# A decoder layer on one core: the last batch's attention finished in two pieces, with alternating PSUM banks

## The reference

```python
gating = jax.nn.softmax(x @ W_gate.T, axis=-1)
idx = jnp.argmax(gating, axis=-1)                 # one of 16 heads per token
k_shared = ...                                    # the chosen head's key, 16 wide
v_shared = ...                                    # its value times its gate
att = jnp.einsum('bhqd,bkd->bhqk', q, k_shared) * (1.0 / math.sqrt(hd))
att = jax.nn.softmax(jnp.where(causal[None, None, :, :], att, -jnp.inf), axis=-1)
y = jnp.einsum('bhqk,bkd->bhqd', att, v_shared)   # 16 heads, one key and value for all
x = _layernorm(x + y, axis=-1)
```

## Time and profile before

| what | value |
|---|---|
| median of 3 runs | 359.49 us (357.77 to 359.7) |
| the profiled execution's own time | 355.84 us |
| its span, first to last instruction | 353.7 us |
| TensorE busy | 315.0 us (89%) |
| VectorE busy | 258.7 us (73%) |
| ScalarE busy | 218.1 us (62%) |
| GpSimd busy | 202.1 us (57%) |
| mean granted TensorE clock | 0.979 |

### The profile page before, as it was taken

How to read it: one execution, slowest core, us unless ns; L and a number is a source line. 1 busy time by engine, 2 the same in 40 slices (tenths; PEclk the granted TensorE clock), 3 DMA queues, 4 the chain that set the end, 5 groups by cost and what they waited for, 6 DMA issues and landing times.

```text
span 353.7 us, 6078 instructions
## 1 busy us (share of the span) xinstructions
PE 315.0 (89%) x2016; PEld 237.1 (67%) x2016; DVE 258.7 (73%) x494; ACT 218.1 (62%) x664; POOL 202.1 (57%) x285
## 2 busy tenths in 40 slices
PE   0949799999999999999999999977779999999972
PEld 0846588778868868877877877855455666666641
DVE  2773984874885794795794595799977989998643
ACT  3638547747655756657657655552347778777781
POOL 0487562775681684582585584299893567922112
PEclk9978999999999999999999999999989999999997
DMA  7921010013000004100004000000000000000001
GB/s 254 330 99 59 3 31 2 1 40 140 1 21 11 2 1 125 56 0 30 2 0 131 1 1 2 0 3 0 0 2 2 2 0 17 19 16 17 0 17 44
DMA packets 5615, 13.06 MB, mean 37 GB/s; under 512 B 849, under 2 KB 3025, under 8 KB 5329
## 3 DMA queue, kind: packets, MB, share of 16 engines
q1 hardware_dynamic: 5040, 11.90, 10.1%
q10 hardware_dynamic: 544, 0.79, 0.7%
HBM read 11.63 MB, written 1.05 MB: 36 GB/s over the span
## 4 chain that ended last, share of the span: by engine, by line
PE 67%; DVE 12%; POOL 10%; issue 5%; DMA 2%; ACT 2%; SPq 1%; POOLq 0%; DVEq 0%; ACTq 0%
PE bank L346 12%; PE bank L467 11%; PE bank L377 8%; PE bank L363 7%; PE bank L456 5%; POOL q_rope L290 4%; DVE toep L999 4%; PE bank L625 4%; PE bank L445 3%; PE bank L614 3%; POOL q_rope L293 3%; PE bank L580 3%; PE bank L635 2%; DMA anti<-in_anti 2%; DVE t_cos L964 2%
## 5 line engine op out<-in xcount | busy, mean ns | idle before, releaser
L1357 POOL TENSOR_TENSOR prob<-prob,rden 128x512 f32<-128x512 f32 x32 | 33.6, 1051 | 69.6 <-DVE rden L1026 69.6
L1336 POOL TENSOR_TENSOR t_sin<-rot,sin 128x512 f32<-128x512 f32 x40 | 54.4, 1360 | 26.4 <-ACT rot L738 23.5
L768 ACT ACTIVATE prob<-bank,neg_max 128x128 f32<-128x128 f32 x128 | 45.3, 369 | 39.1 <-DVE neg_max L1019 39.1
L346 PE MATMUL bank<-x_hi,w_hi 128*128 128x512 f32 x96 | 36.8, 466 | 8.6 <-ACT w_hi L719 8.2
L377 PEld LDWEIGHTS bank<-k_rope,q_rope 128*128 128x128 f32 x256 | 35.0, 200 | 10.5 <-DVE q_rope L977 5.1
L467 PE MATMUL bank<-wo_hi,head_hi 128*128 128x256 f32 x128 | 39.1, 305 | 2.8 <-DVE head_lo L1062 2.7
L377 PE MATMUL bank<-k_rope,q_rope 128*128 128x128 f32 x256 | 35.6, 284 | 4.7 <-DVE q_rope L977 4.7
L894 ACT ACTIVATE prob<-bank,fneg_max 128x128 f32<-128x128 f32 x128 | 36.7, 380 | 2.6 <-DVE fneg_max L1240 2.6
L467 PE MATMUL bank<-wo_lo,head_hi 128*128 128x256 f32 x128 | 36.0, 281 | 0.0
L467 PE MATMUL bank<-wo_hi,head_lo 128*128 128x256 f32 x128 | 35.9, 281 | 0.0
L1326 POOL TENSOR_TENSOR kv<-ctxT 128x256 f32<-128x256 f32 (+3 forms) x64 | 35.2, 585 | 0.0
(11 more groups left out here) (104 smaller groups left out, 743.2 us busy)
## 6 DMA issues: line engine op xcount, KB each, us to landing
w_raw<-in_wqkv SPq DMA_DIRECT2D x3, 768.0 KB, 5.5
toep<-in_toep SPq DMA_DIRECT2D x8, 256.0 KB, 3.3
wo_raw<-in_wo SPq DMA_DIRECT2D x4, 512.0 KB, 3.6
x_raw<-in_xt SPq DMA_DIRECT2D x2, 512.0 KB, 5.9
ctxT<-in_ctx SPq DMA_DIRECT2D x1, 1024.0 KB, 9.1
x<-in_x SPq DMA_DIRECT2D x1, 1024.0 KB, 9.6
out<-x SPq DMA_DIRECT2D x8, 128.0 KB, 1.7
wf<-in_wf SPq DMA_DIRECT2D x1, 784.0 KB, 4.7
```

Of the source, the lines that this page charges most:

```text
L346: last = pe.matmul(out[:, :], wp[:, c, col:col + P], xp[:, j, c, :], start=(c + n == 0), stop=(c == C - 1 and n == 2))
L768: last = act.activation(prob[:, k % 2, h * P:(h + 1) * P], score_bank[k % 2][:, h * P:(h + 1) * P], ACT.Exp, bias=neg_max[:, k % 2, h:h + ...
L1336: pool.tensor_tensor(t_sin[:, par, :].rearrange("p (b t) -> p b t", b=BH), rot[:, par, :].rearrange("p (b t) -> p b t", b=BH), sin[:, :].u ...
L1357: pool.tensor_tensor(own, own, rden[:, k % 2, :].unsqueeze(2).to_broadcast([P, HG, P]), ALU.mult).then_inc(norm_done, 1)
```

## The change

It touches only what comes after `seq(6)` on each engine. The last part, formerly `seq(7)` to `seq(10)`, is written out by hand, with batch 7 treated apart:

- The turns of batch 7 alternate between bank 2 and bank 1 (`tf_bank`); each waits for the copy of the chunk two back.
- Batch 7's chunks 0 to 2 go into bank 0 (`mix_bank`) instead of `y_bank`, chunk 3 into `y_bank`. So chunk 0 no longer waits for `yT_copy(6)`.
- VectorE copies chunk 3's transposed probabilities, not ScalarE.
- The copy, turn, reciprocal and product after that are done in two pieces: heads 0 to 11 (chunks 0 to 2) and heads 12 to 15 (chunk 3), into banks 1 and 2. VectorE adds the state itself, so batch 7 has no `add_ffn` on GpSimd.
- Batch 7's layer norm uses the other set of columns (`stats2`, `mean_var2`, `var_eps2`, `rstd2`).
- `yT_copy(6)` stands behind batch 7's last ScalarE chunk copy, and `y_turn(6)` behind `last_values(2)`. VectorE takes batch 5's statistics ahead of `frow_max(7, 2)`.

```diff
+        def turn_bank(b, c):
+            return tf_bank if b == LAST_B and c % 2 else fprobT_bank
...
-                at_least(pe, fptcopy_done, 4 * b + c, 1)
+                at_least(pe, fptcopy_done, 4 * b + c, 2 if b == LAST_B and c else 1)
...
+            def last_values(c):
+                if c < FC - 1:
+                    pe.wait_ge(fptcopy_done, 4 * LAST_B + c + 1)
+                else:
+                    pe.wait_ge(last_ptcopy_done, 1)
+                    pe.wait_ge(yT_copied, LAST_B)
...
+            def last_y_turn(n):
+                pe.wait_ge(last_yT_copied, n + 1)
+                if n == 0:
+                    pe.wait_ge(last_ptcopy_done, 1)
+                else:
+                    pe.wait_ge(fptcopy_done, 4 * NB - 1)
...
+            def last_yT_copy(n):
+                act.wait_ge(last_yT_done, n + 1)
+                cols = slice(PART[n][0] * P, PART[n][1] * P)
+                act.copy(last_yT[:, cols], last_yT_bank[n][:, cols]).then_inc(last_yT_copied, 1)
...
+            def last_scale(n):
...
+                dve.wait_ge(last_y_done, n + 1)
+                dve.reciprocal(last_yden[:, heads], turned[:, :, FD]).then_inc(last_yden_done, 1)
+                dve.wait_ge(last_yden_done, n + 1)
+                dve.tensor_tensor(own, turned[:, :, 0:FD],
+                                  last_yden[:, heads].unsqueeze(2).to_broadcast([P, wide, FD]), ALU.mult
+                                  ).then_inc(last_ynorm_done, 1)
+                dve.wait_ge(last_ynorm_done, n + 1)
+                last = dve.tensor_tensor(own, own, x[:, LAST_B, :].rearrange("p (h d) -> p h d", d=FD)[:, heads, :],
+                                         ALU.add)
...
             def seq(i):
-                if 0 <= i < NB:
+                if 0 <= i < LAST_B:
                     add_ffn(i)
```

More of the change, by code:

```diff
@@ L141, in decoder_kernel @@
         yT = vT[:, :]
+        last_yT = t_sin[:, 0, :]
+        last_yden = sb("last_yden", [P, FH])
         yden = sb("yden", [P, FH])
@@ L155, in decoder_kernel @@
         mix_bank, tf_bank, kvf_bank, y_bank = bank[0], bank[1], bank[6], bank[7]
+        LAST_B = NB - 1
+        PART = ((0, FC - 1), (FC - 1, FC))
+        last_yT_bank = [mix_bank, y_bank]
+        last_y_bank = [tf_bank, fprobT_bank]
+        def turn_bank(b, c):
+            return tf_bank if b == LAST_B and c % 2 else fprobT_bank
         in_xt = sem("in_xt")
@@ L235, in decoder_kernel @@
         y_done = sem("y_done")
+        last_ptcopy_done = sem("last_ptcopy_done")
+        last_yT_done = sem("last_yT_done")
+        last_yT_copied = sem("last_yT_copied")
+        last_y_done = sem("last_y_done")
+        last_yden_done = sem("last_yden_done")
+        last_ynorm_done = sem("last_ynorm_done")
         yden_done = sem("yden_done")
@@ L622, in fturn @@
                 pe.wait_ge(fexp_done, 4 * b + c + 1)
-                at_least(pe, fptcopy_done, 4 * b + c, 1)
+                at_least(pe, fptcopy_done, 4 * b + c, 2 if b == LAST_B and c else 1)
                 for h in range(4):
-                    last = pe.transpose(fprobT_bank[:, h * P:(h + 1) * P],
+                    last = pe.transpose(turn_bank(b, c)[:, h * P:(h + 1) * P],
                                         prob[:, c % 2, h * P:(h + 1) * P], ident[:, :])
@@ L639, in fvalues @@
                     last.then_inc(yT_done, 1)
+            def last_values(c):
[4 more added lines that the diff above has]
+                    pe.wait_ge(yT_copied, LAST_B)
+                if c == 0:
+                    pe.wait_ge(vext_done, NB)
+                for h in range(4):
+                    last = pe.matmul(last_yT_bank[c // (FC - 1)][h * YW:(h + 1) * YW, c * P:(c + 1) * P],
+                                     vext[:, LAST_B, :], probT[:, c % 2, h * P:(h + 1) * P],
+                                     start=True, stop=True, tile_position=(0, h * YW))
+                if c >= FC - 2:
+                    last.then_inc(last_yT_done, 1)
+            def last_y_turn(n):
[4 more added lines that the diff above has]
+                    pe.wait_ge(fptcopy_done, 4 * NB - 1)
+                for c in range(*PART[n]):
+                    last = pe.transpose(last_y_bank[n][:, c * P:(c + 1) * P],
+                                        last_yT[:, c * P:(c + 1) * P], ident[:, :])
+                last.then_inc(last_y_done, 1)
             def y_turn(b):
@@ L700, in seq @@
                     fscores(i + 1, (i + 1) % 2, 1)
-            for i in range(NB + 1):
+            for i in range(LAST_B):
                 seq(i)
+            fturn(LAST_B, 0)
+            fvalues(LAST_B - 1, 3)
+            fturn(LAST_B, 1)
+            last_values(0)
+            fturn(LAST_B, 2)
+            last_values(1)
+            fturn(LAST_B, 3)
+            last_values(2)
+            y_turn(LAST_B - 1)
+            last_values(3)
+            last_y_turn(0)
+            last_y_turn(1)
         @block.scalar
@@ L899, in fprob_copy @@
                 act.wait_ge(fpt_done, 4 * b + c + 1)
-                act.copy(probT[:, c % 2, :], fprobT_bank[:, :]).then_inc(fptcopy_done, 1)
+                act.copy(probT[:, c % 2, :], turn_bank(b, c)[:, :]).then_inc(fptcopy_done, 1)
             def yT_copy(b):
@@ L952, in seq @@
                     fexps(i, 3)
-            for i in range(NB + 1):
+            for i in range(LAST_B):
                 seq(i)
+            fprob_copy(LAST_B - 1, 2)
+            fexps(LAST_B, 0)
+            fprob_copy(LAST_B - 1, 3)
+            fexps(LAST_B, 1)
+            fprob_copy(LAST_B, 0)
+            fexps(LAST_B, 2)
+            fprob_copy(LAST_B, 1)
+            fexps(LAST_B, 3)
+            fprob_copy(LAST_B, 2)
+            yT_copy(LAST_B - 1)
+            last_yT_copy(0)
+            last_yT_copy(1)
         @block.vector
@@ L1311, in seq, with ffn_norm, ffn_apply @@
                     first_apply(i + 5, (i + 1) % 2)
-            for i in range(NB + 3):
+            for i in range(LAST_B):
                 seq(i)
+            def last_scale(n):
+                heads = slice(4 * PART[n][0], 4 * PART[n][1])
+                wide = heads.stop - heads.start
+                turned = last_y_bank[n][:, :].rearrange("p (h d) -> p h d", h=FH)[:, heads, :]
+                own = ynorm[LAST_B % 2][:, heads, :]
+                dve.wait_ge(last_y_done, n + 1)
[7 more added lines that the diff above has]
+                                         ALU.add)
+                if n == 1:
+                    last.then_inc(ln3[0], 1)
+            def ffn_norm(b):
+                n = 0 if b == LAST_B else 1
+                norm_stats(n, ln3, b, y_flat(b))
+                norm_aggr(n, ln3, b)
+                norm_eps(n, ln3, b)
+            def ffn_apply(b):
+                norm_apply(0 if b == LAST_B else 1, ln3, b, y_flat(b), x[:, b, :])
+            y_invert(LAST_B - 2)
+            y_scale(LAST_B - 2)
+            ffn_apply(LAST_B - 3)
+            frow_max(LAST_B, 0)
+            frow_max(LAST_B, 1)
+            ffn_norm(LAST_B - 2)
+            frow_max(LAST_B, 2)
+            frow_max(LAST_B, 3)
+            ffn_apply(LAST_B - 2)
+            dve.wait_ge(fpt_done, 4 * NB)
+            dve.tensor_copy(probT[:, (FC - 1) % 2, :], turn_bank(LAST_B, FC - 1)[:, :]
+                            ).then_inc(last_ptcopy_done, 1)
+            y_invert(LAST_B - 1)
+            y_scale(LAST_B - 1)
+            last_scale(0)
+            ffn_norm(LAST_B - 1)
+            last_scale(1)
+            ffn_norm(LAST_B)
+            ffn_apply(LAST_B - 1)
+            ffn_apply(LAST_B)
         @block.gpsimd
@@ L1440, in seq @@
                 if 0 <= i < NB:
-                    power(rstd_of[1][:, :], var_eps_of[1][:, :], ln3, i + 1)
+                    n = 0 if i == LAST_B else 1
+                    power(rstd_of[n][:, :], var_eps_of[n][:, :], ln3, i + 1)
                 if 4 <= i + 4 < NB:
```

## The result

The first comparison gave 356.22 us (median of 20 runs, 354.6 to 361.05) against 358.4 us (20 runs, 355.91 to 363.31): a ratio of 0.9939 with a 95% interval of 0.9915 to 0.9962, or 2.2 us less. I had forecast 1.0 us less, and a ratio of 0.9972 lies outside that interval. In the end all runs whose spans are recorded average 357.21 us for the changed kernel (68 runs) and 358.91 us for the one before (110 runs): 1.70 us less, with a standard error of 0.31. The ratios leave out runs over 1.5% above the fastest of their kernel, while the means and groups of spans keep them (without them the means differ by 1.78, with a standard error of 0.24).

What follows compares the result with a forecast made beforehand. The end was taken as a stretch of latencies, hopping between engines for batch 7; −1.27 for chunk 3's turn and +0.28 behind it gave 1.0 us less, 358.5 us against 359.49, range 356.9 to 359.8.

Steps and rivals of the forecast that it cites:

- Steps 1 and 2: Batch 7's turns: with two banks chunk 1's turn goes at 340.71; chunk 3's at 343.65 instead of 344.92, 1.27 earlier.
- Step 3: Batch 6, put behind: `y_turn(6)` done at 345.23, so its finish is 1.5 late and is what VectorE meets first.
- Step 4: Chunk 3 of batch 7: VectorE's copy done at 345.00, its values 345.06 to 345.50, second piece's turn done by 346.2.
- Step 5, first piece: VectorE's queue, heads 0 to 11: reciprocal 345.98, product 346.26, sum from 346.65, held by GpSimd to 347.07 instead of 347.01.
- Step 5, second piece: VectorE's queue, heads 12 to 15: reciprocal at 347.86, 64-column sum held by GpSimd's power to 348.67, last `norm_apply` ending 350.62.
- The sum of the tail: Last `norm_apply` ends at 350.62 instead of 351.61, 1.0 us earlier: −1.27 for chunk 3's turn, +0.28 behind it.
- three signs of being wrong: `y_turn(6)` ending after 345.7; VectorE waiting for the second piece's turn; last store landing over 2.1 us behind the last instruction.
- the first two: Last stores collide, gain vanishes, 359.5 us (chance 0.14); VectorE becomes the bound, slower, about 359.7 us (0.06).
- The rival of a larger gain: At the tail: neither sum held, shorter small copies, earlier exponentials; 1.3 to 2 us gained, 358.0 us; chance 0.18.

## Why the prediction was wrong, point by point

- *Steps 1 and 2, right.* Chunk 1's turn followed 0.95 after the first one (forecast 340.71 − 339.76 = 0.95) and chunk 3's turn 3.89 after it (forecast 3.89). The second bank, without which chunk 3's turn waits, is worth 0.51.
- *Step 3, right.* `y_turn(6)` ended 5.52 after the first turn (forecast 5.47). The kernel with batch 6 early showed that its lateness, with VectorE's part in it, costs 0.85.
- *Step 4, an interval too short.* Chunk 3's values started 0.16 after VectorE's copy ended (347.91 + 0.69 = 348.60 to 348.76), where I had put 0.06. The handover isn't the cause: where TensorE stood idle it was 0.06 (347.04 + 0.69 = 347.73 to 347.79, in the run with batch 6 back in its old place). TensorE's own queue is: the values follow `y_turn(6)` by 348.76 − 348.18 = 0.58, as values follow any turn of 4 blocks in this trace (0.56 to 0.59). I had taken 0.49, the interval from a `y_turn` to another turn, though my own list had 0.56 for a turn with values behind it. This fits that moving chunk 3's copy to ScalarE left the tail at 10.81 and 10.80.
- *Step 5, first piece, two errors that cancel by luck.* By this the first piece was 0.15 late: its sum started 7.04 after the first turn (forecast 346.65 − 339.76 = 6.89). But that sum, which I took as held to 0.2 after GpSimd's end, wasn't held: it started at 350.36, as GpSimd's ended at 350.38. So batch 6's statistics started 7.32 after the first turn (forecast 7.34).
- *Step 5, second piece, two small errors that nearly cancel.* I took the sum of 64 columns as held by the power. It took 0.23 at 351.85, with the power running from 351.54 to 352.09, so it was not held: 0.15 gained. The last power took 0.65 instead of 0.55, beside batch 6's `norm_apply` at 352.86: 0.10 lost.
- *The sum of the tail, right.* 10.80 measured, 10.86 forecast; 1.05 us less against 1.0. None of the three signs of being wrong that I had named showed.
- *The step that failed* is the last one, from the span to the median: "The median of the runs is 3.65 above the profiled execution, and the change touches nothing that would explain that gap". It contained two things. First, I kept the 2.14 between the span and the time unchanged; over all runs it fell from 2.11 to 1.88, so 0.23 us was missing. That makes 1.28 us, a ratio of 0.9964, just outside the first interval (0.9962). Second, I took the scatter of the runs as noise around one value. It isn't. The clock falls to 1.2 GHz somewhere between 240 and 275 us, in other places from run to run, ahead of anything the change touches. In the first profiled execution after, a whole stretch of 10 us was at half of full speed (the stretches' view, PEclk 0.50, third column from the end), where the profiled execution before had 0.83:

```profile
255.00:265.00 10.00, 9.54 (x32) 5.09 (x29) 7.24 (x18) 4.17 (x16) 6.96 (x16) 0.50 0.01 2
```

Two of GpSimd's powers enclose this part, first in the profiled execution before, then after:

```profile
241.58 0.55 POOL L1416 TENSOR_TENSOR rstd<-var_eps,half_pow 128x1 f32<-128x1 f32 x1 [0.34 <-DVE var_eps L1171]
...
277.25 0.55 POOL L1416 TENSOR_TENSOR rstd<-var_eps,half_pow 128x1 f32<-128x1 f32 x1 [8.44 <-DVE var_eps L1171]
```

```profile
241.57 0.55 POOL L1537 TENSOR_TENSOR rstd<-var_eps,half_pow 128x1 f32<-128x1 f32 x1 [0.36 <-DVE var_eps L1244]
...
280.72 0.55 POOL L1537 TENSOR_TENSOR rstd<-var_eps,half_pow 128x1 f32<-128x1 f32 x1 [8.44 <-DVE var_eps L1244]
```

The way between them took 35.67 us before and 39.15 after, 3.48 more, with the same instructions in it; from the second of them to the power at 331.24 (334.80 after) both took 54.0 to 54.1. So nearly all of what makes a span long or short is decided between these two, and the traces fit that the clock decides it, by how long it is low and also by where. In the second trace of the changed kernel the granted share was 1.00 from 255 to 265 and 0.83 from 265 to 275, where the one before had 0.83 and then 1.00, and the way took 37.30.

The second point is seen in the spans of all runs. They can be put in four groups, of which the upper two before aren't sharply parted. Their medians are 354.2, 355.6, 357.65 and 360.15 before (19, 35, 40 and 16 runs) and 352.9, 354.5, 356.6 and 359.2 after (15, 27, 17 and 9 runs). In the first three groups the change is worth 1.3, 1.1 and 1.05 us, about what the tail says. Between the second and third group lies a gap of about 1 us, and the median of the kernel before falls on either side of it from set to set (357.9, 358.1, 359.6 and 359.7 us). So a comparison of medians moves by 2 us and more by where they fall: with the tail fixed at 10.8, the changed kernel's median was 0.6, 1.2 and (twice) 3.0 us below that of its set.

On top of this, 42 of 68 runs after and 54 of 110 before lie in the two lower groups. With equal shares the groups' mean times differ by 1.32 us, and the unequal shares give the other 0.37 of the 1.70. Whether the change made the shorter groups more frequent, or whether it is chance (a difference of 0.13 in the shares, with a standard error of 0.08), is open. No trace shows an instruction ahead of batch 7 that would have moved.

My range (356.9 to 359.8) missed the first median of 356.22, since I put it around a reference of 359.49 that lay in the upper part of the scatter; over 20 runs the reference came out at 358.4. So of the 2.3 us between 358.5 and 356.22, 1.1 are the reference, 0.05 the tail, 0.23 the stretch outside the span, and the remaining 0.9 are not seen in any trace: they lie within the scatter that the later sets showed, and nothing more is shown of them.

Of the rivals, the first two are out: the stretch from the last `norm_apply` to the end of the span was 2.08 after and 2.09 before, so the last stores did not collide, and VectorE's queue cost 0.85 us of the possible gain without making anything slower. The rival of a larger gain described the outcome of the times. One of its mechanisms came true, that neither sum was held, but the 0.15 of the second sum was eaten to 0.05 by the longer last power; what lay beyond the tail was in none of its terms.

## What to carry to other kernels

When a change touches a short end of a long kernel, measure it in the trace from a fixed instruction to the last one: here this repeated to 0.02 us where ratios of the same kernel differed by 0.6%. When a batch is put behind another to clear the critical engine, look at what idles elsewhere: VectorE had 2.9 us free, and giving it batch 6's copy and moving batch 6's finish forward on TensorE and VectorE took 0.85 us more off the tail. Move a step's place on every engine that it passes, since the same turn made early for one queue alone cost 0.38 us.

## What was not expected of the hardware

- GpSimd's sum of 256 columns took 0.72 us at 349.66 and 0.82 us before, where VectorE's `norm_apply` had started 0.16 ahead of it, at 348.68. The last power took 0.65 instead of 0.55 us in the same position. Both fit a GpSimd operation held for 0.1 us by VectorE's instruction in progress. The Trainium skill, "SBUF", section "Who interferes with whom", says that the one that comes second waits; these rows agree in the direction, not in the size, since the instructions overlapped by 0.24 and 0.25, and GpSimd's took 0.10 longer.
- The same rule, taken word for word, would have held the sum of 64 columns at 351.85 until the power's end at 352.09 and some 0.07 on for its columns. It ended at 352.08, in the time that its columns take. Here the row and the rule differ for a power of one column. The sum of 192 columns beside GpSimd's sum of 256 was held (0.72 us, ending 0.22 after it).
- The time of an execution less its span differs between kernels by up to 0.3 us, by a cause that I did not find.
